# Twelve idle tiles hold node rows across stages in a four-layer graph network, and the loops of two node passes become straight code

## The reference

```
x2 = layernorm(x1 + L1(x1, ...))                 # node rows, 50000 x 256
# layer two (graph attention, 8 heads)
ft  = x2 @ W;  e = leaky_relu(a1[src] + a2[dst]);  alpha = softmax of e over the edges of dst
x3 = layernorm(x2 + elu(segment_sum(ft[src] * alpha, dst)))
# layer three (graph attention with self loops, 4 heads)
h   = x3 @ W3.T;  alpha = softmax over edges and the self loop
out = elu(segment_sum(alpha * h[src], dst) + bias) + x3
x   = layernorm(x3 + out)                        # so 2 * x3 + elu(...)
```

## Time and profile before

| | |
|---|---|
| median of 3 runs | 5660.11 us (5659.11 to 5663.49) |
| the profiled execution | 5665.74 us, its span 5664.0 us |
| edge pass of layer two | 3302 to 3872 us of the span |
| node pass | 3872 to 4506 us |
| edge pass of layer three | 4514 to 5038 us |
| last pass | 5038 to 5664 us |
| busy share over the span | PE 74%, DVE 65%, POOL 64%, ACT 35% |
| DMA | 1129.62 MB, mean 199 GB/s |
| mean granted TensorE clock | 0.881 |

### The profile page before, as it was taken

The page is one execution under the profiler, slowest core; times in us unless marked ns, Lnnn a source line. Parts: engine busy times, 40 slices in busy tenths (PEclk is TensorE's granted clock), DMA queues, the critical chain, the costliest instruction groups (busy, mean ns, idle before and its releaser), DMA issues. The chain is left out here.

```text
span 5664.0 us, 69985 instructions
## 1 busy us (share of the span) xinstructions
PE 4214.4 (74%) x16758; PEld 2793.4 (49%) x16758; DVE 3700.9 (65%) x10195; ACT 1961.5 (35%) x3345; POOL 3614.0 (64%) x3312
## 2 busy tenths in 40 slices
PE   2277669989999999999999967875778500036666
PEld 1155435556666666666666657764666400012222
DVE  2155456656665666666666657777999665558888
ACT  0011135532222222222222222225888500026666
POOL 7488644433455655555555557774888777768887
PEclk6688889999999999999999988887999855569888
DMA  9988789975433333333333234446999733349998
GB/s 378 286 156 156 143 272 366 366 292 185 145 126 111 114 127 115 122 115 116 119 123 113 91 111 139 137 145 219 350 349 352 252 102 94 95 162 355 344 338 298
DMA packets 497174, 1129.62 MB, mean 199 GB/s; under 512 B 164006, under 2 KB 246906, under 8 KB 497030
## 3 DMA queue, kind: packets, MB, share of 16 engines
q1 hardware_dynamic: 331530, 866.20, 43.6%
q0 software_dynamic: 113184, 174.84, 12.8%
q10 hardware_dynamic: 52316, 87.06, 4.4%
HBM read 627.40 MB, written 543.83 MB: 207 GB/s over the span
## 5 line engine op out<-in xcount | busy, mean ns | idle before, releaser
L1018 PE MATMUL psum<-arena,W1b 128*128 128x512 f32 x1568 | 727.5, 607 | 0.0
L1041 PE MATMUL psum<-W2b,arena 128*128 128x256 f32 x3136 | 725.6, 379 | 2.5 <-DVE arena L974 2.5
L773 DVE TENSOR_SCALAR arena<-arena 128x256 f32<-128x256 f32 x784 | 462.4, 651 | 363.3 <-POOL arena L768 363.3
L1041 PEld LDWEIGHTS psum<-W2b,arena 128*128 128x128 f32 x3136 | 573.1, 190 | 69.7 <-issue 3.9
L1735 PE MATMUL psum<-arena,ident 128*128 128x512 f32 x784 | 412.7, 676 | 209.4 <-POOL arena L1793 207.3
L931 ACT ACTIVATE arena<-psum,hbias 128x512 f32<-128x512 f32 x392 | 269.4, 687 | 863.1 <-PE psum L1018 863.1
L764 POOL TENSOR_TENSOR arena<-arena,lneps 128x4 f32<-128x4 f32 x196 | 39.8, 203 | 731.4 <-DVE arena L760 730.5
L1018 PEld LDWEIGHTS psum<-arena,W1b 128*128 128x128 f32 x1568 | 282.5, 190 | 432.0 <-issue 432.0
L1166 POOL DMA_INDIRECT tab<-arena,IDX x392 | 406.7, 1037 | 122.0 <-issue 89.9
L1584 POOL DMA_INDIRECT ad_d<-arena,FE x392 | 394.8, 1007 | 114.2 <-issue 113.9
L891 POOL DMA_INDIRECT xd_d<-arena,FE x360 | 379.0, 1053 | 97.4 <-issue 97.1
(11 more groups left out here) (248 smaller groups left out, 9297.0 us busy)
## 6 DMA issues: line engine op xcount, KB each, us to landing
arena<-tab SPq DMA_DIRECT2D x194, 544.0 KB
arena<-x_d SPq DMA_DIRECT2D x202, 512.0 KB, 6.8
arena<-in_x SPq DMA_DIRECT2D x194, 512.0 KB, 3.8
x_d<-arena SPq DMA_DIRECT2D x194, 512.0 KB, 2.9
tab<-zero SPq DMA_DIRECT2D x11, 5832.0 KB, 54.5
tab<-blank SPq DMA_DIRECT2D x97, 544.0 KB
h_d<-arena SPq DMA_DIRECT2D x97, 528.0 KB, 6.0
arena<-h_d SPq DMA_DIRECT2D x97, 528.0 KB, 5.5
```

The source lines that it names most:

```text
L773: v.tensor_scalar(y[:, j, :], r[:, j, :], self.mv[:, j, 0:1], self.rs[:, j:j + 1], ALU.subtract, ALU.mult).then_inc(self.s["y"], 1)
L1018: last = pe.matmul(psum[:, BR + c % RING, :], W1b[:, f, c * P:(c + 1) * P], x1T[:, f, :], start=False, stop=(f == FH - 1))
L1041: last = pe.matmul(outB(j), hid[:, c, j * P:(j + 1) * P], W2b[:, c, :], start=(c == 0), stop=(c == KH - 1))
```

## The change

Three things change.

**Where rows are kept.** Twelve tiles of 128 x 1024 floats that are idle in the last four stages are collected in `spare`: the weights of layers zero and one, the attention vectors, the zero and the blank tile, and five tiles at the end of the arena. For that, some small tiles are allocated as one.

**Which transfers are made.** In the edge pass of layer two, SP issues twelve loads of x2 (steps 4 to 15 of the node pass) right behind the first four `xd` loads; they land in the spare tiles. The node pass then loads no `xt` for these steps. Steps 20, 26, 32, ..., 86 of the node pass write their normed tile into a spare tile and not into `y`; it isn't stored to x3, and the last pass reads it there and loads nothing for that step.

**How the steps are written.** In the node pass, SP, PE, ACT and DVE, and in the last pass SP and DVE, no longer use `run_beats` but a plain loop in Python, so that all 98 steps are straight code with constant targets and addresses. POOL, PE and ACT of the last pass keep their hardware loops.

```diff
+        NSP = 12
+        SPARE0 = ARENA - 5 * J * D
+        spare = [tile_of(W1b[:, :, :], "p f d -> p (f d)"), tile_of(W2b[:, :, :], "p f d -> p (f d)"),
+                 tile_of(Wa[:, :, :, :], "p a f d -> p (a f d)"), tile_of(Weu[:, :, :], "p a d -> p (a d)"),
+                 tile_of(att23[:, :, :, :], "p l a d -> p (l a d)"), tile_of(zero[:, :], "p d -> p d"),
+                 tile_of(blank[:, :, :], "p j c -> p (j c)")]
+        spare += [arena[:, SPARE0 + i * J * D:SPARE0 + (i + 1) * J * D]... for i in range(5)]
+        EARLY0 = NB
+        KEPT = {20 + 6 * i: i for i in range(NSP)}
+        STRAIGHT = NB * NS
@@ edge_pass, g_sync
-                run_beats(sp, CS, body, NG, start=S0)
+                for s in range(S0, S0 + NG):
+                    body(beat(s, NG))
+                ahead["early", L](sp)
+                run_beats(sp, CS - NG, body, NG, start=S0 + NG)
                 ahead["rows", L](sp)
@@ node_pass
             def rows(sp, k):
                 b = k.slot(NB)
-                wait(sp, r["r"], k.s - NB + 1)
+                if k.s >= EARLY0 + NSP:
+                    wait(sp, r["r"], k.s - NB + 1 if k.s >= EARLY0 + NSP + NB else k.s - NB - NSP + 1)
                 a, n = node_view(xin, k)
-                sp.dma_start(xt[0:n, b, :, :], a).then_inc(n_x[b], 16)
+                sp.dma_start(xtile(k)[0:n, :, :], a).then_inc(n_x[b], 16)
@@ node_pass, store
                     sp.wait_ge(r["y"], J * (k.s + 1))
+                    if k.s in KEPT:
+                        return
@@ node_pass, normed
+                    if k.s in KEPT:
+                        act.wait_ge(r["r"], EARLY0 + KEPT[k.s] + 1)
@@ node_pass, the same for PE, ACT and SP
-                run_beats(v, NS, body, NB, peel=NB + 1)
+                for s in range(NS):
+                    body(beat(s, STRAIGHT))
@@ last_pass, the same for SP
-                run_beats(v, NS, body, NB)
+                for s in range(NS):
+                    body(beat(s, STRAIGHT))
```

More of the change, by code:

```diff
@@ L1493, in body @@
                     b = k.slot(NB)
-                    if not (k.known() and k.s < NB):
+                    if k.s >= EARLY0 + NSP:
                         rows(sp, k)
@@ L1562, in body @@
                         relu_exp(k.plus(1))
-                    if not (k.known() and k.s < 2):
+                    if k.s >= 2:
                         normed(k.plus(-2))
-                    if not (k.known() and k.s < 3):
+                    if k.s >= 3:
                         evac(k.plus(-3))
-                run_beats(act, NS, body, NB, peel=2 * NB)
+                for s in range(NS):
+                    body(beat(s, STRAIGHT))
                 for s in range(NS - 2, NS):
-                    normed(beat(s, NB))
-                    evac(beat(s - 1, NB))
-                evac(beat(NS - 1, NB))
+                    normed(beat(s, STRAIGHT))
+                    evac(beat(s - 1, STRAIGHT))
+                evac(beat(NS - 1, STRAIGHT))
             def n_gpsimd(pool):
@@ L1618, in body @@
                                                in1=tt[:, k.slot(NB), 2 * i:2 * i + 2, 0:D], op0=ALU.add, op1=ALU.max).then_inc(r["elu"], 1)
-                    if b == 0 and not (k.known() and k.s == 0):
+                    if b == 0 and k.s > 0:
                         shift(k.plus(-2))
@@ L1638, in body @@
                         v.tensor_tensor(out=ve, in0=mv[:, k.slot(NB) // 2, :, 1], in1=lneps[:, :], op=ALU.add).then_inc(r["ve"], 1)
-                    if not (k.known() and k.s < 4):
+                    if k.s >= 4:
                         to_rows(k.plus(-4))
-                run_beats(v, NS, body, NB, peel=NB + 1)
-                shift(beat(NS - 2, NB))
+                for s in range(NS):
+                    body(beat(s, STRAIGHT))
+                shift(beat(NS - 2, STRAIGHT))
                 for s in range(NS - 4, NS):
-                    to_rows(beat(s, NB))
+                    to_rows(beat(s, STRAIGHT))
             return n_sync, n_scalar, n_gpsimd, n_vector, n_tensor
@@ L1685, in pair_cols, with loaded, xtile @@
                 return t[:, b:b + 2, :, c:c + H].rearrange("p s j h -> p (s j) h")
+            def loaded(k):
+                return 16 * (k.turn(NB) + 2 * USES[k.slot(NB)] + 1 - kept_before(k.s, k.slot(NB)))
+            def xtile(k):
+                if k.s in KEPT:
+                    return spare[KEPT[k.s]]
+                return xt[:, k.slot(NB), :, :]
             def rows(sp, k):
                 b = k.slot(NB)
-                if not (k.known() and k.s < NB):
+                if k.s in KEPT:
+                    return
+                if k.s >= NB:
                     sp.wait_ge(r["r"], k.s + Z - NB + 1)
@@ L1722, in body @@
                         tables(k.plus(NB + 3))
[L1723 removed]
+                for s in range(NS):
+                    body(beat(s, STRAIGHT))
                 for b in range(NB):
[L1725 removed]
+                    sp.wait_ge(n_w[b], sent(NS, b) + 16 * USES[b])
             def l_tensor(pe):
```

78 lines of the change are left out of this document (48 added, 30 removed).

## The result

The changed kernel took **5679.2 us** (median of 6 runs, 5676.27 to 5687.12), the kernel before on the same chip 5660.14 us (6 runs): ratio 1.0038, 95% interval 1.0028 to 1.0049. It is slower by 19 us, outside the forecast range and on its other side.

A forecast was written before the change was run, and what follows sets the result against it. It took POOL to bound the node pass and a circle of DVE, POOL, PE and ACT, led partly by DVE, the last pass; 0 + 0 + 3 - 11 - 2 = -10 us gave 5650 us, range 5622 to 5668.

The forecast's parts named there:

- Transfers out of the node pass: Node pass: dropping twelve loads and twelve stores saves 0 us, as nobody waits for them; ends 0 and -36.
- Rival B: Node and last pass: DMA is the bound after all, so 36 and 18 us go; 5609 us, chance 0.06.
- Straight code in the node pass: Node pass: SP, PE, ACT and DVE lose register work but have slack to POOL; 0 us.
- Early loads: Start of layer two's edge pass: twelve loads share DMA with POOL's first gathers; +3 us, ends 0 and +17.
- Straight code in the last pass: Last pass: 0.42 us less in each of 27 looped steps that DVE leads; -11 us, ends 0 and -37.
- the circle: Last pass: the chain DVE, POOL, PE, ACT, DVE, said to lead the steps DVE does not, 5.98 us each.
- Transfers out of the last pass: Last pass: twelve loads (6.3 MB) fewer, DVE's waits for `tab` being 3.3 us; -2 us, ends 0 and -18.
- A: Last pass: it keeps its 5.98 us rhythm whatever DVE gives back; 5661 us, chance 0.18.
- C: Last pass: DVE leads nearly always, so all looped steps gain 0.42 us; 5624 us, chance 0.15.
- D: Last pass: straight DVE code arrives late through full DMA; 5698 us, chance 0.13 with milder form or late edge-pass start.
- E: Whole change: the transfers are not saved, SP issuing as many as before; ruled out from SP's order, no chance given.

The follow-up runs named there:

- e4: Changed kernel with loops put back in both passes, kept tiles moved to steps 8 to 19, longer straight heads; ratio 1.0000 to the kernel before.
- e14: Changed kernel, last pass looped, kept steps 8 to 19, eight added matmuls a last-pass step, two statistics instructions every second node-pass step; 0.9976 to the kernel before.
- e15: Kernel before, all transfers kept, node pass straight with two statistics instructions every second step, eight added matmuls a last-pass step; ratio 0.9971.
- e2: Kernel before with only the node pass straight (SP, PE, ACT, DVE), on a 5820 us kind of chip; ratio 0.9976.
- e6: Kernel before with only DVE's loop of the last pass unrolled; ratio 1.0027, last pass 644.9 us.
- e7: Kernel before with only SP's loop of the last pass unrolled; ratio 1.0003, last pass 633.8 us.
- e10: Changed kernel with eight added matmuls in every step of the last pass; ratio 1.0011 to the kernel before, last pass 625.1 us.
- e11: Kernel before with eight added matmuls in every step of the last pass; ratio 0.9984, last pass 613.3 us.
- e16: Kernel before with only DVE's loop of the node pass unrolled; ratio 1.0004, node pass 635.4 us.
- e13: Changed kernel with two statistics instructions ahead of DVE's elu in every second node-pass step; ratio 1.0011 to the kernel before, node pass 625.8 us.
- e9: Changed kernel with six one-column memsets added to every DVE step of the last pass; ratio 1.0042 to the kernel before, last pass 636.4 us.

## Why the prediction was wrong

**Transfers out of the node pass, 0 us: right.** e4 gives 1.0000, e14 and e15 differ by 0.0005, and 21 GB/s less left POOL busy from end to end as before. Rival B is out.

**Straight code in the node pass, 0 us: wrong, +7.3 us.** This step failed in kind. Its reason, "all of them have slack to POOL", was true, and it was taken to mean that nothing they do can matter, so the step had no ends at all. But slack lets an engine move in time, and where it stands decides how long POOL's own instruction takes. The rows had it: a mean of 1892 ns that is the mean of 1.69 and 2.11, and a DVE that waits for exactly this instruction 27 times. On the other kind of chip the same step was a gain of 0.24% (e2), for POOL had gaps there.

**Early loads, +3 us: right.** From POOL's first gather to PE's first transposes there were 8.6 us, now 11.3, so +2.7, and POOL's wait for ACT grew from 7.30 to 10.04 us. PE's timeline of after, against the earlier trace rows:

```profile
3308.96 1.94 PE L1219 MATMUL psum<-ident,arena 128*128 128x128 f32 x8 [31.46 <-DMA arena<-x_d,IDX]
```

The gathers did not wait for all twelve loads: that would be 17 us by the estimate from 366 GB/s, and the delay is 2.7. Why it lies near the low end no run shows.

**Straight code in the last pass, -11 us: wrong, +11.3 us.** The size of a step was right: 5.44 us wherever DVE follows itself, 28 times. The 11 us were multiplied out as if the other steps kept their length. They did not: after each short step two longer ones follow, DVE waits 76.3 us for ACT instead of 27.4, and 14 steps are over 7 us instead of 3. The end at 0, "if the circle closes at once", was not an end; a loss had been left out for no reason that a row gave. e6 and e7 put it on DVE's code alone, on the other kind of chip. How a quicker DVE makes the circle slower, by its rhythm or by the clock that it brings down, was not separated and stays open.

**Transfers out of the last pass, -2 us: about right.** DVE's wait for `tab` fell from 3.3 to 1.4 us; no run has this term alone.

**The clock, without a term in the sum: missed.** The granted clock fell from 0.91 to 0.86 and the matmuls took 700 instead of 676 ns. Keeping TensorE busy gave 12 to 13 us back in the traces of e10 and e11; how much of the loss of the last pass is the clock's stays open.

**Rivals.** A (the circle takes all) names the right place and stops short: it takes more than all. C is out: its steps came, its gain did not. D forecast "slower", for a reason that did not occur: from 5050 us to the end the instruction queues q8 and q14 moved 22 packets in after and 6 in before, and DVE's waits for issue sum to 0.7 us. E is out.

## What to carry to other kernels

An engine with slack is not free to change: where its instructions run beside those of the engine that sets the pace, look at that engine's own durations (1.69 us or 2.03 to 2.19 for POOL's power here), and where one instruction has two lengths in the trace, ask what stands beside it. In a circle over several engines, do not multiply a saving by the steps in which one engine leads; give such a term an end on the losing side. And where TensorE waits some us a step (1.4 and 4.4 here) in a stage that follows its pace, work that nobody needs can be worth more than work removed: it gave 0.16% in e11.

## What the runs showed of the hardware

- POOL's 128x8 power instruction takes 1.69 us alone. If DVE's elu, 128x512 with both inputs in SBUF, begins 0.19, 0.11 or 0.02 us ahead of it, it takes 2.03, 2.11 and 2.19 us. Each time it ends 1.48 to 1.53 us after the first of the elu's two instructions (0.69 us) does. From 0.10 us behind it takes 1.69 us; between 0.05 and 0.08 us behind either happens, 2.25 us twice and 1.69 us twelve times (e16). Statistics instructions in the same place (one input) leave it at 1.69 us (e13).
- In the last pass DVE's 128x32 instructions with both inputs in SBUF, 0.19 us alone, take mostly 1.77 to 1.95 us when they begin just behind the start of POOL's 128x1024 one (1.90 us). DVE's 128x1024 instructions with one input in PSUM meet it over 100 times a trace and take 1.22 us as ever.
- It matters who begins first. In the last pass of e10, DVE's 128x32 instructions that begin 0.02 to 0.67 us behind the start of POOL's 128x1024 one end 0.05 us behind its end; those that begin ahead of it take 0.19 us. In the node pass the elu that begins first makes the power instruction longer, 2.03 to 2.19 us as above. But POOL's power instruction does not hold DVE back for its whole length: an elu that begins 0.29 us or more behind it runs inside its 1.69 us and takes 0.68 to 0.69 us, as it does ahead of it (before, e13), and one that begins 0.05 to 0.08 us behind takes at most 0.75 (e16). Why the two POOL instructions differ no run shows.
- Six memsets of one column a step made DVE's short steps 0.03 us longer (e9), so they are no delay. Two statistics instructions of 256 and 128 columns moved the elu by 0.5 us.
- Eight added matmuls a step (16 of 128 columns in the trace, 1.95 us together, where 1.1 was expected) raised the granted clock of the last pass from 0.91 to 0.99 (e11) and made it 13 us shorter.
- One program takes 5660 us on some chips and 5820 on others, with the edge passes 1.11 to 1.14 times as long at a granted clock of 0.79 instead of 0.85. The straight node pass is a loss of 7 us on the first and a gain of 0.24% on the second. Why is open.
